# Cross attention on one Trainium2 core: values as three one-pass products, low parts of the exponents on GpSimd

## The chip, the cores and the metric

One core of one Trainium2 chip runs the whole program. The metric is the device time of one execution in microseconds (us), the median over several runs.

## The reference

Two post-norm decoder layers on x of 4 x 512 x 512 in float32: `x = layernorm(x + f(x))` for six f in turn. The change is in the fifth, the second layer's cross attention to `ctx_1024` (4 x 512 x 256), with 16 heads of 128:

```python
q = (hidden_states @ Wq).reshape(B, Sq, H, D)
k = (encoder_hidden_states @ Wk).reshape(B, Skv, H, D)
v = (encoder_hidden_states @ Wv).reshape(B, Skv, H, D)
q = rmsnorm(q, gq)
k = rmsnorm(k, gk)
scores = jnp.einsum('bqhd,bkhd->bhqk', q, k) * scale
attn = jax.nn.softmax(scores, axis=-1)
out = jnp.einsum('bhqk,bkhd->bqhd', attn, v)
return out.reshape(B, Sq, H * D) @ Wo
```

## The kernel before

`cross_attention` works on two heads at a time (`HP = 2`); with 8 such pairs in each of 4 batch entries there are N = 32 pairs, numbered j. A float32 operand `a` of most products is split into `a_hi`, rounded to float32r by ScalarE, and `a_lo = a - a_hi`, made by VectorE or GpSimd. `split3` (L196 to L200) then makes one float32 product out of three one-pass products: hi x hi, hi x lo, lo x hi. A plain float32 product takes four passes and shows as two records.

The order of the work is one list, `seq`, written out by hand in a loop over j. Every engine walks the same list and does its part of each step, so each engine's queue has the steps in the list's order. In round j three pairs are in work: the attention of pair j (`now`), the projections of pair j+1 (`nxt`) and the output of pair j-1 (`prv`). The steps are:

- E(j, h, k): scores of key block k in TensorE; ScalarE's exponent into `probs` (L1936), scaled by the keys' `rs` of GpSimd.
- U(j, h): GpSimd adds the four blocks of `probs` (L1868, L1870, L1872); SU(j, h): TensorE sums over partitions with a product by ones in bank 7 (L2111); R and M: VectorE's reciprocal (L2010) and the product with the values' result (L2015).
- V(j, h): `v` by `probs`, four float32 products (L2104) into bank 5 + h.
- Q(j, i): the two halves of the queries' projection; ScalarE squares (L1904) and copies (L1907). MQ: VectorE's mean square (a reduction L1964, a tensor_scalar L1967), then GpSimd's power -1/2 (L1843), the rstd. NQ: VectorE scales the queries in place (L1993).
- KV(j, t): keys and values of token block t; ScalarE squares, copies the keys and copies the values to `v` (L1921), which frees the bank. MK: the keys' mean square and rstd.
- TQ, TK(j, h): TensorE turns queries and keys (L2045), ScalarE takes the high part (L1925), VectorE the low part (L2000, L2003), which frees the bank.
- OH(j, h): high (L1943) and low part (L2020) of the attention's output. O(j, t): output projection, which VectorE adds to `x` (L2025).
- WQ, WK, WO: ScalarE's high parts of the next weights (L1892, L1895, L1898); GpSimd's low parts at WQ, WKl, WOl (L1849, L1853, L1857). After each low part SP loads the next weights into the one raw buffer.

Banks: Q, KV, TK and TQ take turns in banks 0 and 1, E and O in 2 to 4, V in 5 and 6, SU in 7. Before the change KV2 takes the bank of KV1, as TQ0 stands between them in the order of use:

```python
            if s[0] in ("Q", "KV", "TK", "TQ") or s[0] == "X" and s[2] % 2:
                uses.append((s, na % 2, 1))
                na += 1
```

Of the kernel before, what the change touches and what calls it, by code (L numbers as in the profile page):

```python
# [20 lines left out]
P = 128  # L21
B, S, D = 4, 512, 512
T = S // P
# [8 lines left out]
DX = 128  # L32
# [1605 lines left out]
def cross_attention(c):  # L1638
# [11 lines left out]


    nc, d, ps = c.nc, c.d, c.ps
    HP = 2
# [3 lines left out]
    with ExitStack() as ctx:  # L1657
# [21 lines left out]
        kk = sb("k", [P, T, NW])  # L1679
        v = sb("v", [P, T, NW])  # L1680
        sq = c.xcur[:, 0:2, :].rearrange("p a (b n) -> p (a b) n", n=NW)
# [4 lines left out]
        f_l = sb("qkT_lo", [P, 2, HP, S], F32R)  # L1686
        probs = sb("probsT", [P, HP, T, S])
        inv = sb("inv_sums", [P, HP, S])
        o_h = sb("outT_hi", [P, HP, S], F32R)
# [10 lines left out]
        x_hi, ctx_hi, ctx_lo = cnt("x_hi", KD), cnt("ctx_hi"), cnt("ctx_lo")  # L1700
        squared = {"q": cnt("q_squared"), "k": cnt("k_squared")}
        ms_ready = {"q": cnt("q_mean_sq"), "k": cnt("k_mean_sq")}
        rs_ready = {"q": cnt("q_rstd"), "k": cnt("k_rstd")}
        q_normed = cnt("q_normed")
        f_hi = {"TK": cnt("kT_hi", HP), "TQ": cnt("qT_hi", HP)}
        p_sum, o_hi, o_lo = cnt("probs_summed", HP), cnt("out_hi", HP), cnt("out_lo", HP)
        var_ready, rstd_ready, nmr_ready = cnt("ln_var"), cnt("ln_rstd"), cnt("ln_shift")
# [5 lines left out]
        for j in range(-1, N + 1):  # L1713
            now, nxt, prv, border = 0 <= j < N, j + 1 < N, 0 <= j - 1, (j + 2) % G == 0 and j + 2 < N
            if now:
                seq += [("E", j, 0, k) for k in range(T)] + [("U", j, 0)]
            if nxt:
                seq.append(("Q", j + 1, 0))
            if now:
                for k in range(T):  # L1720
                    seq.append(("E", j, 1, k))
                    if prv and k < HP:
                        seq.append(("OH", j - 1, k))
                seq += [("U", j, 1), ("V", j, 0)]
            elif prv:
                seq += [("OH", j - 1, h) for h in range(HP)]
            if j + 2 < N:
                seq.append(("WQ", j + 2))
            if nxt:
                if (j + 1) % G == 0 and j > 0:  # L1730
                    seq.append(("Cx", (j + 1) // G))
                seq += [("Q", j + 1, 1), ("MQ", j + 1)]
            if now:
                seq += [("SU", j, 0), ("R", j, 0)]
            if j + 2 < N:
                seq.append(("WK", j + 2))
            if now:
                seq.append(("WO", j))
            if border:
                seq += [("X", (j + 2) // G, k) for k in range(KD)]  # L1740
            if j % G == 1 and j > G:
                seq.append(("LX", j // G - 1))
            if nxt:
                seq.append(("NQ", j + 1))
            if now:
                seq.append(("M", j, 0))
            if prv:
                seq.append(("O", j - 1, 0))
            if now:
                seq.append(("V", j, 1))  # L1750
            if nxt:
                seq.append(("KV", j + 1, 0))
            if now:
                seq.append(("SU", j, 1))
            if nxt:
                seq += [("KV", j + 1, 1), ("TQ", j + 1, 0), ("KV", j + 1, 2)]
            if j + 2 < N:
                seq.append(("WKl", j + 2))
            if now:
                seq.append(("WOl", j))  # L1760
            if prv:
                seq.append(("O", j - 1, 1))
            if nxt:
                seq += [("TQ", j + 1, 1), ("KV", j + 1, 3), ("MK", j + 1)]
            if prv:
                seq.append(("O", j - 1, 2))
            if nxt:
                seq.append(("TK", j + 1, 0))
            if prv:
                seq.append(("O", j - 1, 3))  # L1770
            if nxt:
                seq.append(("TK", j + 1, 1))
            if now:
                seq += [("R", j, 1), ("M", j, 1)]
            if prv and j % G == 0:
                seq.append(("L", j // G - 1))
# [3 lines left out]
        for s in seq:  # L1780
            if s[0] in ("Q", "KV", "TK", "TQ") or s[0] == "X" and s[2] % 2:
                uses.append((s, na % 2, 1))
# [4 lines left out]
            elif s[0] == "V":  # L1787
                uses.append((s, 5 + s[2], 1))
            elif s[0] == "SU":
                uses.append((s, 7, 1))  # L1790
# [49 lines left out]
        def _(pool):  # L1840
            def rstd(i, nm, j):
                pool.wait_ge(*ms_ready[nm].after(j, 1))
                pool.tensor_tensor(rs[:, i, :, :], ms[:, i, :, :], c.mhalf[:, 0:T * HP].rearrange("p (t h) -> p t h", h=HP),  # L1843
                                   ALU.pow).then_inc(rs_ready[nm].sem, 1)

            for ph, j, *s in seq:
# [16 lines left out]
                elif ph == "U":  # L1863
# [8 lines left out]
                    pool.tensor_tensor(psum[:, h, :], psum[:, h, :], probs[:, h, 3, :], ALU.add).then_inc(p_sum.sem, 1)  # L1872
                    pool.drain()
                elif ph == "L":
                    pool.wait_ge(*var_ready.after(j, 1))
# [3 lines left out]
        def _(act):  # L1879
            for ph, j, *s in seq:  # L1880
# [15 lines left out]
                elif ph == "WO":  # L1896
                    act.wait_ge(*rawo_in.after(j, 16))
                    act.activation(side(wo_h, j), raw_o[:, :], ACT.Copy).then_inc(wo_hi.sem, 1)  # L1898
                elif ph == "Q":
                    i = s[0]  # L1900
                    act.wait_ge(*ps.full(0, ("Q", j, i)))
                    if j > 0:
                        act.wait_ge(*ms_ready["k"].after(j - 1, 1))
                    sqr = act.activation(sq[:, 2 * i:2 * i + 2, :].rearrange("p a n -> p (a n)"), ps.ap(("Q", j, i)), ACT.Square)  # L1904
                    if i == 1:
                        sqr.then_inc(squared["q"].sem, 1)
                    act.activation(q[:, 2 * i:2 * i + 2, :].rearrange("p a n -> p (a n)"), ps.ap(("Q", j, i)), ACT.Copy) \  # L1907
                       .then_inc(ps.freed(("Q", j, i)), 1)
                elif ph == "KV":
# [3 lines left out]
                    if t == 0:  # L1913
                        act.wait_ge(*ms_ready["q"].after(j, 1))
                    sqr = act.activation(sq[:, t, :], kv[:, 0:NW], ACT.Square)  # L1915
                    if t == T - 1:
                        sqr.then_inc(squared["k"].sem, 1)
                    act.activation(kk[:, t, :], kv[:, 0:NW], ACT.Copy)
                    if j > 0 and t == 0:
                        act.wait_ge(*ps.full(0, ("V", j - 1, 1)))  # L1920
                    act.activation(v[:, t, :], kv[:, NW:], ACT.Copy).then_inc(ps.freed(("KV", j, t)), 1)  # L1921
                elif ph in ("TK", "TQ"):
# [4 lines left out]
                elif ph == "E":  # L1927
                    h, k = s
                    if h == 0 and k == 0:
                        act.wait_ge(bound_ready, 1)  # L1930
                        act.wait_ge(*rs_ready["k"].after(j, 1))
                    if k == 0 and j > 0:
                        act.wait_ge(*p_sum.after(j - 1, h + 1))
                        act.wait_ge(*ps.full(0, ("V", j - 1, h)))
                    act.wait_ge(*ps.full(0, ("E", j, h, k)))
# [15 lines left out]
        def _(dve):  # L1951
# [10 lines left out]
            def mean_squares(i, nm, j):  # L1962
                dve.wait_ge(*squared[nm].after(j, 1))
                dve.tensor_reduce(ms[:, i, :, :], sq.rearrange("p t (h n) -> p t h n", h=HP), AX.X, ALU.add)  # L1964
                dve.drain()
                per = (1.0 / DX, 1e-5) if nm == "q" else (1.0, 1e-5 * DX)
                dve.tensor_scalar(ms[:, i, :, :], ms[:, i, :, :], per[0], per[1], ALU.mult, ALU.add) \  # L1967
                   .then_inc(ms_ready[nm].sem, 1)

            for ph, j, *s in seq:  # L1970
# [18 lines left out]
                elif ph == "NQ":  # L1989
                    dve.wait_ge(*rs_ready["q"].after(j, 1))  # L1990
                    dve.wait_ge(*ps.released(0, ("Q", j, 1)))
                    x3 = q[:, :, :].rearrange("p t (h n) -> p (t h) n", h=HP)
                    dve.tensor_tensor(x3, x3, rs[:, 0, :, :].rearrange("p t h -> p (t h)").unsqueeze(2)  # L1993
                                      .broadcast_to([P, T * HP, DX]), ALU.mult).then_inc(q_normed.sem, 1)
                elif ph in ("TK", "TQ"):
                    h = s[0]
# [44 lines left out]
        def _(pe):  # L2041
# [6 lines left out]
            for ph, j, *s in seq:  # L2048
# [48 lines left out]
                elif ph == "V":  # L2097
                    h = s[0]
                    ps.wait_empty(pe, 0, key)
                    if h == 0:  # L2100
                        pe.wait_ge(*ps.released(0, ("KV", j, T - 1)))
                    for k in range(T):
                        pe.wait_ge(*ps.released(0, ("E", j, h, k)))
                        mm = pe.matmul(ps.ap(key), v[:, k, h * DX:(h + 1) * DX], probs[:, h, k, :],  # L2104
                                       start=(k == 0), stop=(k == T - 1))
                    mm.then_inc(ps.filled(key), 1)
# [600 lines left out]
```

## Time and profile before

| | us |
|---|---|
| median of 3 runs | 2547.98 (2547.49 to 2548.07) |
| the profiled execution, its own time | 2548.6 |
| its span, first to last instruction | 2546.8 |
| cross attention, first to last copy of output weights (L1898, one a pair) | 1208.4 to 2246.1 |
| TensorE busy over the span | 2188.1 (86%) |
| VectorE, ScalarE, GpSimd busy over the span | 1422.8, 1224.2, 932.3 |

PE is TensorE's matmul, PEld its weight load, DVE VectorE, ACT ScalarE, POOL GpSimd, SP SyncE. Rows of a timeline give start, duration, engine, line, operation, output<-input, count, and in brackets the idle time before with what ended it. TensorE's products are pipelined and their ends are modelled, so prices of products are taken from start to start. The mean granted clock of TensorE over the span is 0.948 of full speed.

### The profile page before, as it was taken

What the parts mean: (1) busy time and instruction counts of PE and PEld (TensorE: products, weight loads), DVE (VectorE), ACT (ScalarE), POOL (GpSimd) and SP (SyncE); (2) the same over time, 40 slices, a digit from 0 to 9 for tenths busy, and PEclk for the clock granted to TensorE, in tenths of its full rate; (3) what the DMA queues carried; (4) which work ended last, traced back from release to release, by engine and by line L of the source; (5) the groups of instructions that cost most, each with busy time, mean ns of one, the idle gap of its engine ahead of it and who ended that gap; (6) DMA issues with size and microseconds to landing.
All of it is one profiled execution on the core that took longest, in us unless ns stands there. A gap on an engine that the chain in (4) does not pass through costs nothing. (4 is left out here: it accounts for less than half of the span.)

```text
span 2546.8 us, 33202 instructions
## 1 busy us (share of the span) xinstructions
PE 2188.1 (86%) x12629; PEld 1551.4 (61%) x12664; DVE 1422.8 (56%) x2129; ACT 1224.2 (48%) x2321; POOL 932.3 (37%) x662
## 2 busy tenths in 40 slices
PE   5989899857896787797999999999999999976781
PEld 4555556436675665555677777777777777753340
DVE  3656666635555435543566665566666655652637
ACT  3636464523424636544555555555555555541413
POOL 2525252410003202203555555555555655520101
PEclk9999999978997999998999999999999999988786
DMA  3000000010001000002111111111111111011001
GB/s 110 1 1 1 1 1 1 1 63 1 1 1 49 1 1 1 1 2 80 47 50 50 58 50 50 42 39 53 50 50 50 50 50 45 20 46 56 1 1 66
DMA packets 60550, 79.12 MB, mean 31 GB/s; under 512 B 6052, under 2 KB 40228, under 8 KB 60392
## 3 DMA queue, kind: packets, MB, share of 16 engines
q1 hardware_dynamic: 60392, 76.99, 9.0%
q8 instruction: 102, 1.67, 0.3%
q14 instruction: 56, 0.46, 0.1%
HBM read 72.78 MB, written 4.19 MB: 30 GB/s over the span
## 5 line engine op out<-in xcount | busy, mean ns | idle before, releaser
L2104 PE MATMUL banks<-s_probsT,s_v 128*128 128x512 f32 x512 | 230.1, 592 | 0.0
L594 DVE TENSOR_REDUCE s_neg_max<-banks 128x1 f32<-128x512 f32 x256 | 165.5, 685 | 89.4 <-PE banks L660 87.9
L2010 DVE RECIPROCAL s_inv_sums<-banks 128x512 f32<-128x512 f32 x64 | 214.2, 3347 | 1.2 <-PE banks L2111 1.2
L1843 POOL TENSOR_TENSOR s_qk_rstd<-s_mean_sq,minus_half 128x8 f32<-128x8 f32 x64 | 105.2, 1643 | 249.2 <-DVE s_mean_sq L1967 246.1
L1936 ACT ACTIVATE s_probsT<-banks,s_minus_bound,s_qk_rstd 128x512 f32<-128x512 f32 x256 | 186.3, 785 | 11.2 <-PE banks L200 11.2
L543 ACT ACTIVATE s_probsT<-banks 128x512 f32<-128x512 f32 x256 | 148.8, 600 | 81.4 <-PE banks L674 79.1
L1964 DVE TENSOR_REDUCE s_mean_sq<-x_cur 128x8 f32<-128x1024 f32 x64 | 78.1, 1220 | 185.5 <-ACT x_cur L1904 174.3
L198 PE MATMUL banks<-s_w_proj_hi,xT_hi 128*128 128x256 f32 x512 | 158.3, 309 | 2.9 <-DVE s_w_proj_lo L1987 2.9
L2104 PEld LDWEIGHTS banks<-s_probsT,s_v 128*128 128x128 f32 x512 | 96.9, 189 | 97.9 <-issue 92.4
L1915 ACT ACTIVATE x_cur<-banks 128x256 f32<-128x256 f32 x128 | 49.3, 385 | 219.3 <-PE banks L200 219.1
L1868 POOL TENSOR_TENSOR x_cur<-s_probsT 128x512 f32<-128x512 f32 x64 | 82.3, 1286 | 193.3 <-ACT s_probsT L1936 193.1
L198 PE MATMUL banks<-s_w_proj_hi,s_ctxT_hi 128*128 128x512 f32 x256 | 131.5, 514 | 19.4 <-ACT s_v L1921 19.4
L199 PE MATMUL banks<-s_w_proj_lo,xT_hi 128*128 128x256 f32 x512 | 145.8, 285 | 0.0
L200 PE MATMUL banks<-s_w_proj_hi,xT_lo 128*128 128x256 f32 x512 | 145.7, 285 | 0.0
L482 POOL TENSOR_TENSOR x_cur<-s_probsT 128x512 f32<-128x512 f32 x64 | 82.1, 1282 | 158.2 <-PE banks L692 109.9
L660 PE MATMUL banks<-s_kT,s_qT 128*128 128x512 f32 x256 | 118.4, 468 | 6.8 <-ACT s_qT L532 3.2
L2025 DVE TENSOR_TENSOR x_all<-banks,x_all 128x512 f32<-128x512 f32 x128 | 87.7, 685 | 60.3 <-PE banks L200 58.5
L1904 ACT ACTIVATE x_cur<-banks 128x512 f32<-128x512 f32 x64 | 38.2, 598 | 171.6 <-PE banks L200 171.6
L674 PE MATMUL banks<-s_qT,s_kT 128*128 128x512 f32 x256 | 106.3, 415 | 16.4 <-ACT s_qT L536 14.3
L198 PE MATMUL banks<-s_w_out_hi,s_outT_hi 128*128 128x512 f32 x256 | 115.6, 451 | 5.5 <-DVE s_outT_lo L2020 5.5
L198 PE MATMUL banks<-s_wqkv_hi,xT_hi 128*128 128x512 f32 (+1 forms) x256 | 92.1, 360 | 29.0 <-POOL s_wqkv_lo L464 8.8
L198 PE MATMUL banks<-s_qkT_hi 128*128 128x512 f32 x256 | 105.8, 413 | 2.8 <-DVE s_qkT_lo L2003 2.8
(417 smaller groups left out, 6156.5 us busy)
## 6 DMA issues: line engine op xcount, KB each, us to landing
s_w_proj_raw<-l1x_wq SPq DMA_DIRECT2D x32, 512.0 KB, 3.3
s_w_out_raw<-l1x_wo SPq DMA_DIRECT2D x32, 512.0 KB, 3.6
s_w_proj_raw<-l1x_wk SPq DMA_DIRECT2D x32, 256.0 KB, 2.8
s_w_proj_raw<-l1x_wv SPq DMA_DIRECT2D x32, 256.0 KB, 3.1
x_all<-x SPq DMA_DIRECT2D x4, 1024.0 KB, 12.7
s_ctxT<-ctxT SPq DMA_DIRECT2D x8, 512.0 KB, 4.9
out<-x_all SPq DMA_DIRECT2D x4, 1024.0 KB, 4.3
s_probsT<-l0a_wqkv SPq DMA_DIRECT2D x1, 1536.0 KB, 9.4
```

The costliest lines, as they stand in the source:

```text
L198: pe.matmul(out, lhs[0], rhs[0], start=start, stop=False)
L199: pe.matmul(out, lhs[0], rhs[1], start=False, stop=False)
L200: return pe.matmul(out, lhs[1], rhs[0], start=False, stop=stop)
L543: act.activation(probsT[:, h % NPB, k, :], ps.ap(s), ACT.Exp).then_inc(ps.freed(s), 1)
L594: dve.tensor_reduce(nmax[:, h % 2, t, 0:1], ps.ap(s), AX.X, ALU.max, negate=True) \
L660: pe.matmul(ps.ap(s), qT[:, h % NQB, t * P:(t + 1) * P], kT[:, h % NKV, :], start=True, stop=True).then_inc(ps.filled(s), 1)
L674: pe.matmul(ps.ap(s), kT[:, h % NKV, k * P:(k + 1) * P], qT[:, h % NQB, :], start=True, stop=True).then_inc(ps.filled(s), 1)
L1843: pool.tensor_tensor(rs[:, i, :, :], ms[:, i, :, :], c.mhalf[:, 0:T * HP].rearrange("p (t h) -> p t h", h=HP), ALU.pow).then_inc(rs_ready[ ...
L1936: act.activation(probs[:, h, k, :], ps.ap(("E", j, h, k)), ACT.Exp, bias=bound[:, 0:1], scale=rs[:, 1, k, h:h + 1]).then_inc(ps.freed(("E" ...
L2010: dve.reciprocal(inv[:, h, :], ps.ap(("SU", j, h))).then_inc(ps.freed(("SU", j, h)), 1)
L2025: dve.tensor_tensor(xt, ps.ap(("O", j, t)), xt, ALU.add).then_inc(ps.freed(("O", j, t)), 1)
L2104: mm = pe.matmul(ps.ap(key), v[:, k, h * DX:(h + 1) * DX], probs[:, h, k, :], start=(k == 0), stop=(k == T - 1))
```

## The change

1. The values' product becomes three one-pass products for each key block. `v` is kept as `v_hi` (ScalarE's copy) and `v_lo` (a new VectorE subtraction at KV, which now frees the bank). The exponents are kept as `probs` and, for one head at a time, `p_h` (a ScalarE copy of two blocks, 128x1024, at the new step PH) and `p_l` (a GpSimd subtraction of the same size, at the new step PL). In V the eight products with `p_h` come first, then the four with `p_l`. A head's first PH waits until the values before it in the same buffer are done.
2. U(j, 1) goes behind the second half of the queries and the rstd; WQ behind that. SU(j, 1) goes behind KV3 and MK.
3. TQ(j, 0) goes into bank 7, between the two sums.
4. Three pairs of semaphores (q and k) become one each, counted twice a round.

```diff
+        v_h = sb("v_hi", [P, T, NW], F32R)
+        v_l = sb("v_lo", [P, T, NW], F32R)
...
+        p_h = sb("probsT_hi", [P, T, S], F32R)
+        p_l = sb("probsT_lo", [P, T, S], F32R)
...
             if now:
-                seq += [("E", j, 0, k) for k in range(T)] + [("U", j, 0)]
+                for k in range(T):
+                    seq.append(("E", j, 0, k))
+                    if k % 2:
+                        seq += [("PH", j, 0, k // 2), ("PL", j, 0, k // 2)]
+                seq.append(("U", j, 0))
...
-                seq += [("U", j, 1), ("V", j, 0)]
+                seq.append(("V", j, 0))
+                for i in range(2):
+                    seq += [("PH", j, 1, i), ("PL", j, 1, i)]
             elif prv:
                 seq += [("OH", j - 1, h) for h in range(HP)]
-            if j + 2 < N:
-                seq.append(("WQ", j + 2))
             if nxt:
                 if (j + 1) % G == 0 and j > 0:
                     seq.append(("Cx", (j + 1) // G))
                 seq += [("Q", j + 1, 1), ("MQ", j + 1)]
+            if now:
+                seq.append(("U", j, 1))
+            if j + 2 < N:
+                seq.append(("WQ", j + 2))
...
-            if nxt:
-                seq.append(("KV", j + 1, 0))
-            if now:
-                seq.append(("SU", j, 1))
-            if nxt:
-                seq += [("KV", j + 1, 1), ("TQ", j + 1, 0), ("KV", j + 1, 2)]
+            if j < 0:
+                seq += [("KV", 0, 0), ("KV", 0, 1), ("KV", 0, 2), ("KV", 0, 3), ("TQ", 0, 0)]
+            elif nxt:
+                seq += [("KV", j + 1, 0), ("KV", j + 1, 1), ("TQ", j + 1, 0)]
+            if nxt and now:
+                seq.append(("KV", j + 1, 2))
...
             if nxt:
-                seq += [("TQ", j + 1, 1), ("KV", j + 1, 3), ("MK", j + 1)]
+                seq.append(("TQ", j + 1, 1))
+                if now:
+                    seq.append(("KV", j + 1, 3))
+                seq.append(("MK", j + 1))
+            if now:
+                seq.append(("SU", j, 1))
...
-            if s[0] in ("Q", "KV", "TK", "TQ") or s[0] == "X" and s[2] % 2:
+            if s[0] in ("Q", "KV", "TK") or s[0] == "TQ" and s[2] or s[0] == "X" and s[2] % 2:
...
-            elif s[0] == "SU":
+            elif s[0] in ("SU", "TQ"):
                 uses.append((s, 7, 1))
...
+                elif ph == "PL":
+                    h, i = s
+                    k2 = slice(2 * i, 2 * i + 2)
+                    pool.wait_ge(*p_hi.after(j, 2 * h + i + 1))
+                    pool.tensor_tensor(p_l[:, k2, :], probs[:, h, k2, :], p_h[:, k2, :].bitcast(F32), ALU.subtract) \
+                        .then_inc(p_lo.sem, 1)
...
+                elif ph == "PH":
+                    h, i = s
+                    k2 = slice(2 * i, 2 * i + 2)
+                    if i == 0 and j + h > 0:
+                        act.wait_ge(*ps.full(0, ("V", j, 0) if h else ("V", j - 1, 1)))
+                    act.wait_ge(*ps.released(0, ("E", j, h, 2 * i + 1)))
+                    act.activation(p_h[:, k2, :], probs[:, h, k2, :], ACT.Copy).then_inc(p_hi.sem, 1)
...
-                    act.activation(v[:, t, :], kv[:, NW:], ACT.Copy).then_inc(ps.freed(("KV", j, t)), 1)
+                    act.activation(v_h[:, t, :], kv[:, NW:], ACT.Copy).then_inc(v_hi.sem, 1)
...
                     if k == 0 and j > 0:
                         act.wait_ge(*p_sum.after(j - 1, h + 1))
-                        act.wait_ge(*ps.full(0, ("V", j - 1, h)))
+                        act.wait_ge(*p_lo.after(j - 1, 2 * h + 2))
...
+                elif ph == "KV":
+                    t = s[0]
+                    dve.wait_ge(*v_hi.after(j, t + 1))
+                    dve.tensor_tensor(v_l[:, t, :], ps.ap(("KV", j, t))[:, NW:], v_h[:, t, :].bitcast(F32), ALU.subtract) \
+                       .then_inc(ps.freed(("KV", j, t)), 1)
...
+                    cols = slice(h * DX, (h + 1) * DX)
                     for k in range(T):
-                        pe.wait_ge(*ps.released(0, ("E", j, h, k)))
-                        mm = pe.matmul(ps.ap(key), v[:, k, h * DX:(h + 1) * DX], probs[:, h, k, :],
-                                       start=(k == 0), stop=(k == T - 1))
+                        if k % 2 == 0:
+                            pe.wait_ge(*p_hi.after(j, 2 * h + k // 2 + 1))
+                        pe.matmul(ps.ap(key), v_h[:, k, cols], p_h[:, k, :], start=(k == 0), stop=False)
+                        pe.matmul(ps.ap(key), v_l[:, k, cols], p_h[:, k, :], start=False, stop=False)
+                    for k in range(T):
+                        if k % 2 == 0:
+                            pe.wait_ge(*p_lo.after(j, 2 * h + k // 2 + 1))
+                        mm = pe.matmul(ps.ap(key), v_h[:, k, cols], p_l[:, k, :], start=False, stop=(k == T - 1))
                     mm.then_inc(ps.filled(key), 1)
```

## Rows read from the trace of the kernel before

**Rows 1.** Busy time in one round: stretch, length, engines (instructions), TensorE's clock, DMA.

```profile
1799.10:1832.60 33.50, 32.91 (x157) 24.51 (x156) 19.65 (x20) 17.72 (x33) 19.04 (x12) 1.00 0.15 47
```

**Rows 2.** Line L1898: count, shortest/median/longest ns, first and last start.

```profile
L1898 ACT ACTIVATE s_w_out_hi<-s_w_out_raw x32: 1055/1056/1062, 1208.4 to 2246.1; 128x1024 fp32r<-128x1024 f32 x32
```

**Rows 3.** Timeline of TensorE in that round (start us, us, instruction, idle before).

```profile
1802.69 0.28 PE L198 MATMUL banks<-s_w_proj_hi,xT_hi 128*128 128x256 f32 x1
...
1805.56 0.40 PE L198 MATMUL banks<-s_qkT_hi 128*128 128x512 f32 x1
...
1806.26 0.40 PE L198 MATMUL banks<-s_qkT_hi 128*128 128x512 f32 x1
...
1808.38 3.59 PE L2104 MATMUL banks<-s_probsT,s_v 128*128 128x512 f32 x8
...
1811.92 0.28 PE L199 MATMUL banks<-s_w_proj_lo,xT_hi 128*128 128x256 f32 x1
...
1825.17 0.50 PE L198 MATMUL banks<-s_w_proj_hi,s_ctxT_hi 128*128 128x512 f32 x1 [0.59 <-ACT s_v L1921]
...
1833.44 0.47 PE L198 MATMUL banks<-s_qkT_hi 128*128 128x512 f32 x1
```

**Rows 4.** Timeline of ScalarE in that round.

```profile
1800.91 2.79 ACT L1936 ACTIVATE s_probsT<-banks,s_minus_bound,s_qk_rstd 128x512 f32<-128x512 f32 x4 [0.18 <-PE banks L200]
...
1814.88 0.60 ACT L1904 ACTIVATE x_cur<-banks 128x512 f32<-128x512 f32 x1 [3.37 <-PE banks L200]
...
1834.50 2.12 ACT L1936 ACTIVATE s_probsT<-banks,s_minus_bound,s_qk_rstd 128x512 f32<-128x512 f32 x3 [0.18 <-PE banks L200]
```

**Rows 5.** Timeline of VectorE in that round.

```profile
1816.80 0.56 DVE L1967 TENSOR_SCALAR s_mean_sq<-s_mean_sq 128x8 f32<-128x8 f32 x1
1817.28 3.34 DVE L2010 RECIPROCAL s_inv_sums<-banks 128x512 f32<-128x512 f32 x1
1820.54 1.96 DVE L1993 TENSOR_TENSOR s_q<-s_q,s_qk_rstd 128x1024 f32<-128x1024 f32 x1
1822.43 0.68 DVE L2015 TENSOR_TENSOR s_inv_sums<-banks,s_inv_sums 128x512 f32<-128x512 f32 x1
1823.03 0.68 DVE L2025 TENSOR_TENSOR x_all<-banks,x_all 128x512 f32<-128x512 f32 x1
...
1831.76 0.17 DVE L1967 TENSOR_SCALAR s_mean_sq<-s_mean_sq 128x8 f32<-128x8 f32 x1
```

**Rows 6.** Timeline of GpSimd in that round.

```profile
1810.64 1.27 POOL L1868 TENSOR_TENSOR x_cur<-s_probsT 128x512 f32<-128x512 f32 x1 [2.70 <-ACT s_probsT L1936]
...
1814.94 2.39 POOL L1849 TENSOR_TENSOR s_w_proj_lo<-s_w_proj_raw,s_w_proj_hi 128x1024 fp32r<-128x1024 f32 x1 [0.16 <-issue]
1817.44 1.65 POOL L1843 TENSOR_TENSOR s_qk_rstd<-s_mean_sq,minus_half 128x8 f32<-128x8 f32 x1
1819.06 2.37 POOL L1853 TENSOR_TENSOR s_w_proj_lo<-s_w_proj_raw,s_w_proj_hi 128x1024 fp32r<-128x1024 f32 x1
1821.38 3.37 POOL L1857 TENSOR_TENSOR s_w_out_lo<-s_w_out_raw,s_w_out_hi 128x1024 fp32r<-128x1024 f32 x1
1832.01 1.64 POOL L1843 TENSOR_TENSOR s_qk_rstd<-s_mean_sq,minus_half 128x8 f32<-128x8 f32 x1 [7.26 <-DVE s_mean_sq L1967]
```

**Rows 7.** Timeline of VectorE in the last pair.

```profile
2244.11 3.37 DVE L2020 TENSOR_TENSOR s_outT_lo<-s_inv_sums,s_outT_hi 128x512 fp32r<-128x512 f32 x2
```

**Rows 8.** Timeline of GpSimd in the last pair.

```profile
2245.39 1.53 POOL L1872 TENSOR_TENSOR x_cur<-x_cur,s_probsT 128x512 f32<-128x512 f32 x1
```

**Rows 9.** DMA issues: KB each, median us from issue to landing.

```profile
s_w_proj_raw<-l1x_wq SPq DMA_DIRECT2D x32, 512.0 KB, 3.3
```

**Rows 10.** Timeline of TensorE in the second pair.

```profile
1220.82 1.09 PE L2045 MATMUL banks<-ident_sb,s_k 128*128 128x128 f32 x8 [1.02 <-ACT s_v L1921]
1222.89 0.79 PE L198 MATMUL banks<-s_qkT_hi 128*128 128x512 f32 x1 [0.97 <-DVE s_qkT_lo L2003]
```

**Rows 11.** Busy time and granted clock behind that wait, columns as in rows 1.

```profile
1223.00:1226.00 3.00, 3.00 (x7) 2.37 (x8) 3.00 (x2) 0.92 (x2) 0.44 (x1) 0.50 0.00 0
```

More of the change, by code:

```diff
@@ L1679, in cross_attention @@
         kk = sb("k", [P, T, NW])
-        v = sb("v", [P, T, NW])
+        v_h = sb("v_hi", [P, T, NW], F32R)
+        v_l = sb("v_lo", [P, T, NW], F32R)
         sq = c.xcur[:, 0:2, :].rearrange("p a (b n) -> p (a b) n", n=NW)
@@ L1700, in cross_attention @@
         x_hi, ctx_hi, ctx_lo = cnt("x_hi", KD), cnt("ctx_hi"), cnt("ctx_lo")
-        squared = {"q": cnt("q_squared"), "k": cnt("k_squared")}
-        ms_ready = {"q": cnt("q_mean_sq"), "k": cnt("k_mean_sq")}
-        rs_ready = {"q": cnt("q_rstd"), "k": cnt("k_rstd")}
+        squared = cnt("qk_squared", 2)
+        ms_ready, rs_ready, nth = cnt("qk_mean_sq", 2), cnt("qk_rstd_ready", 2), {"q": 1, "k": 2}
         q_normed = cnt("q_normed")
         f_hi = {"TK": cnt("kT_hi", HP), "TQ": cnt("qT_hi", HP)}
+        p_hi, p_lo, v_hi = cnt("probs_hi", 2 * HP), cnt("probs_lo", 2 * HP), cnt("v_hi", T)
         p_sum, o_hi, o_lo = cnt("probs_summed", HP), cnt("out_hi", HP), cnt("out_lo", HP)
@@ L1841, in rstd @@
             def rstd(i, nm, j):
-                pool.wait_ge(*ms_ready[nm].after(j, 1))
+                pool.wait_ge(*ms_ready.after(j, nth[nm]))
                 pool.tensor_tensor(rs[:, i, :, :], ms[:, i, :, :], c.mhalf[:, 0:T * HP].rearrange("p (t h) -> p t h", h=HP),
-                                   ALU.pow).then_inc(rs_ready[nm].sem, 1)
+                                   ALU.pow).then_inc(rs_ready.sem, 1)
             for ph, j, *s in seq:
@@ L1902, in _ @@
                     if j > 0:
-                        act.wait_ge(*ms_ready["k"].after(j - 1, 1))
+                        act.wait_ge(*ms_ready.after(j - 1, nth["k"]))
                     sqr = act.activation(sq[:, 2 * i:2 * i + 2, :].rearrange("p a n -> p (a n)"), ps.ap(("Q", j, i)), ACT.Square)
                     if i == 1:
-                        sqr.then_inc(squared["q"].sem, 1)
+                        sqr.then_inc(squared.sem, 1)
                     act.activation(q[:, 2 * i:2 * i + 2, :].rearrange("p a n -> p (a n)"), ps.ap(("Q", j, i)), ACT.Copy) \
@@ L1913, in _ @@
                     if t == 0:
-                        act.wait_ge(*ms_ready["q"].after(j, 1))
+                        act.wait_ge(*ms_ready.after(j, nth["q"]))
                     sqr = act.activation(sq[:, t, :], kv[:, 0:NW], ACT.Square)
                     if t == T - 1:
-                        sqr.then_inc(squared["k"].sem, 1)
+                        sqr.then_inc(squared.sem, 1)
                     act.activation(kk[:, t, :], kv[:, 0:NW], ACT.Copy)
@@ L1930, in _ @@
                         act.wait_ge(bound_ready, 1)
-                        act.wait_ge(*rs_ready["k"].after(j, 1))
+                        act.wait_ge(*rs_ready.after(j, nth["k"]))
                     if k == 0 and j > 0:
                         act.wait_ge(*p_sum.after(j - 1, h + 1))
-                        act.wait_ge(*ps.full(0, ("V", j - 1, h)))
+                        act.wait_ge(*p_lo.after(j - 1, 2 * h + 2))
                     act.wait_ge(*ps.full(0, ("E", j, h, k)))
@@ L1962, in mean_squares @@
             def mean_squares(i, nm, j):
-                dve.wait_ge(*squared[nm].after(j, 1))
+                dve.wait_ge(*squared.after(j, nth[nm]))
                 dve.tensor_reduce(ms[:, i, :, :], sq.rearrange("p t (h n) -> p t h n", h=HP), AX.X, ALU.add)
@@ L1967, in mean_squares @@
                 dve.tensor_scalar(ms[:, i, :, :], ms[:, i, :, :], per[0], per[1], ALU.mult, ALU.add) \
-                   .then_inc(ms_ready[nm].sem, 1)
+                   .then_inc(ms_ready.sem, 1)
             for ph, j, *s in seq:
@@ L1989, in _ @@
                 elif ph == "NQ":
-                    dve.wait_ge(*rs_ready["q"].after(j, 1))
+                    dve.wait_ge(*rs_ready.after(j, nth["q"]))
                     dve.wait_ge(*ps.released(0, ("Q", j, 1)))
```

## The prediction

> **What bounds the kernel now.** I read the busy time of one round of the cross attention first (a round: one pair of heads; 32 pairs, 31 rounds from the first pair's to the last pair's). In 33.50 us TensorE is busy 32.91 at a granted clock of 1.00; VectorE has 19.65, ScalarE 17.72, GpSimd 19.04 [rows 1]. So TensorE sets the round. Over the stage the same line returns 31 times between 1208.4 and 2246.1, 33.5 us each [rows 2].
>
> TensorE's own timeline then gives prices as steps from start to start, since its ends are modelled [rows 3]. A half of the queries (24 products of 256 columns) takes 1805.56 - 1802.69 = 2.87 us, 0.12 each. Three one-pass products of 512 columns take 1806.26 - 1805.56 = 0.70, 0.233 each. A head's values begin at 1808.38; the second product behind them starts at 1811.92, so the values end at 1811.92 - 0.12 = 11.80 and cost **3.42 us** for 8 records, or 0.86 for 2, which is also what one sum (SU) costs. The one wait in the round is 0.59 before the third KV block.
>
> The other engines' timelines tell who could take over. I count from a pair's first exponent, 1800.91 [rows 4], in round times. In these the second Q half reaches ScalarE at 14.0, the mean square's tensor_scalar starts at 15.9, the query scaling (NQ, L1993) runs 19.6 to 21.6, and the next pair's first exponent is at 1834.50, so this round is 33.6 [rows 4, 5].
>
> **VectorE and GpSimd block each other** in these rows. The tensor_scalar, ready at 1816.80, takes 0.56 instead of the 0.17 it takes when GpSimd idles: it ends as GpSimd's subtraction of 2.39 us does. NQ starts at 1820.54 in GpSimd's L1853, which ends at 1821.43, and ends 1.07 later; GpSimd's next one, L1857, takes 3.37 where L1853 takes 2.37, so it lost 1.0 [rows 5, 6]. L2015, with one operand in PSUM, takes 0.68 in the midst of L1857: no conflict [rows 5, 6]. In the last pair two low parts of the output (L2020) meet the adds: 3.37 us for two, and the add beside them 1.53 [rows 7, 8], some 0.25 lost to GpSimd for each (1.53 against 1.27 in [rows 6]).
>
> **The change, part by part.**
>
> 1. Values on TensorE: 12 one-pass products replace a four-pass chain, 12 x 0.233 = 2.80 against 3.42, so 0.62 less a head and 1.24 a pair [rows 3]. The wait of 0.59 goes too, since queries turned in bank 7 leave KV2 another bank. TensorE alone would run at 33.5 - 1.24 - 0.59 = 31.7. Weights for the extra products load beside the products before, as those of the 0.233 steps do.
>
> 2. ScalarE copies the exponents' high parts (PH): 4 a pair, 128x1024 from SBUF, the form of L1898 at 1.06 us [rows 2]. That is 4.2 us on top of 17.72 of 33.50 [rows 1]; the engine has room. On the path only the first counts (below).
>
> 3. VectorE's four low parts of the values: no row has 128x256. The 128x512 product from PSUM is 0.68 [rows 5]; bounds are half of that and the whole, 0.34 to 0.68. I take 0.35, half of that row for half of its columns. With one operand in PSUM it meets no port [rows 5, 6]. Only KV0's lies on the path, since it frees KV2's bank; at the upper bound a round gains 0.3.
>
> 4. GpSimd's low parts of the exponents (PL): four subtractions of the form and size of L1849 and L1853, 2.37 to 2.39 us, 9.5 a pair [rows 6]. This is the large term. Old GpSimd stood idle 7.26 before the keys' rstd and 2.70 before the second sum [rows 6].
>
> 5. Moved: U1 (three adds, 1814.94 - 1810.64 = 4.30 us [rows 6]) goes behind the queries' rstd, so WQ, WKl, WOl run later. SP waits for each of these before it loads the next weights; a load lands after 3.3 us [rows 9], and ScalarE wants it most of a round later: nothing. WQ's copy on ScalarE goes behind Q1: nothing. SU1 goes behind KV3, 0.86 inside the stretch from KV2 to the next scores. The merged semaphores cost nothing, as the waits are the same.
>
> **GpSimd's order, added up.** From the first exponent: two exponents (2.79 for four [rows 4], some 1.45 for two) and the first PH (1.06) pass before PL can start, at 2.6. Then PL, PL 4.75; U0 4.3; PL, PL 4.75; a wait of 0.2 for the tensor_scalar; queries' rstd 1.62; U1 4.3; WQ, WKl, WOl 7.1; keys' rstd 1.62. Sum 31.2. With the port's losses (two L2020 at 0.25, NQ 1.0, tensor_scalar 0.2) it is 32.9. So GpSimd is full as well, and whoever of VectorE wants the port finds it taken.
>
> **The chain I forecast.** V0 starts at 7.5 as before and ends at 10.3 (PL01 ends at 7.45, in time). Q1 reaches ScalarE 3.08 after V0's end, as 1814.88 - 1811.80 [rows 3, 4], at 13.35, and the tensor_scalar is ready 1.92 later (1816.80 - 1814.88 [rows 4, 5]), at 15.3. GpSimd has U0 from 7.45 to 12.25 (with 0.5 lost), PL10 to 14.6, PL11 to 17.0. The tensor_scalar misses the gap at 14.6 by 0.7 and stands until 17.0. Behind it in VectorE's queue is the reciprocal, 3.26 to the next start [rows 5], 17.1 to 20.4, and then NQ. U1's adds run from 18.85 (rstd 17.2 to 18.85), the second from 20.3: NQ finds the port taken just before it, waits to 21.6 and ends at 22.65. KV2 needs KV0's bank, whose low part stands in VectorE's queue behind NQ, M0 and O0: 0.6 + 0.6 (L2015 to the next start [rows 5]) + 0.35, and 0.15 to TensorE (less than half of the 0.36 by which 1834.50 - 1833.44 exceeds three products), so KV2 starts at 24.4. TensorE was through KV1 at 20.8 (PL11 at 17.0, four products, two KV blocks of 1.4), and stands except for one turn. From KV2 to the next scores it took 1833.44 - 1825.17 = 8.27; with SU1 9.13; from scores to exponent 1834.50 - 1833.44 = 1.06 [rows 3, 4]. Round: 24.4 + 9.13 + 1.06 = **34.6**, against 33.6: 1.0 longer.
>
> Bounds: if NQ slips in ahead of the second add it is 1.1 earlier, but then the keys' tensor_scalar (ready at 30.8) stands behind WOl (to 31.3), the keys' low parts behind it, and the round is 34.0. With the values' low part at 0.68 it is 34.9. So 34.0 to 34.9; I take 34.6, nearest to the rows' order. 31 rounds x 1.0 = 31 us. The execution profiled took 2548.6 (span 2546.8, 1.8 around it), 0.6 above the median of 2547.98. Forecast 2548.6 + 31 = **2580**, own range 2561 to 2592.
>
> **Rivals.**
>
> *TensorE stays the bound (faster).* If the port conflicts fall into GpSimd's gaps and the tensor_scalar gets in before PL11, the round is between TensorE's 31.7 and GpSimd's 32.9; at 32.5 the time is 2548.6 - 31 x 1.1 = 2514. For it: TensorE has by far the most work, and the sum of GpSimd's order is below 33.6. Against: GpSimd leaves no gap in which VectorE could go first. It decides from the point where NQ ends before 33.6 - (34.6 - 22.65) = 21.65 and the keys' tensor_scalar no longer waits behind WOl. Chance 0.16.
>
> *Even.* GpSimd's order plus a little of the chain, 33.4 to 33.7; the gain on TensorE is given back exactly: 2542 to 2552. Chance 0.12.
>
> *The clock falls in the new wait.* In the second pair TensorE stood 1.02 and 0.97 us around eight turns, and the granted clock behind was 0.50 for 3 us [rows 10, 11], that is 1.2 of 2.4 GHz. The wait from 20.8 to 24.4, with four turns in it, is like that one. Three us at half speed lose 1.5, so with one in each round 36.1 and 2548.6 + 31 x 2.5 = 2626. Against: the 0.59 waits of each old round leave the clock at 1.00 [rows 1, 3]. Chance 0.20.
> The Trainium skill ("TensorE: Matmul & The Clock Gate", Part 1) says that half speed is the default state and only activity lifts it; by that rule a stand of this kind in every round would cost in every round, and the time would be the 2626 of this rival. The trace of before has the one case.
>
> *The exponents' low parts are slower than L1853,* or the one buffer for both heads holds the second head back: PL10 waits for V0's end (10.3 + 0.2 + 1.06 = 11.6) but GpSimd is in U0 until 12.25, so this costs nothing until V0 is 0.7 late. It is within the forecast's range.
>
> **How the numbers follow.** Chances: forecast 0.52, clock 0.20, faster 0.16, even 0.12. 0.2% (5 us) is about what a measurement of this kernel can tell from no change. Faster is 0.16, same 0.12, slower 0.52 + 0.20 = 0.72. The range goes down to 2530, which leaves out most of the faster case (0.12), and up to 2640, one and a half of the clock's falls in some rounds, which leaves out 0.06.
>
> **What would show it.** Right: L2104's successors in steps of 0.23; GpSimd near 29 us busy a round; the queries' tensor_scalar (L1967) far above the 0.56 of [rows 5], ending with PL11; NQ ending 22 to 23 after the first exponent; TensorE waiting before the queries' turn and KV2 for VectorE; a round of 34 to 35. Wrong: a round below 33.3 with NQ early, or GpSimd idle for several us before the keys' rstd. The clock rival shows as a granted clock clearly below 1.00 in the stage.

## The result, and the profile after

| | before | changed |
|---|---|---|
| median, us | 2548.03 | 2571.51 (2570.22 to 2572.57) |
| span of the profiled execution | 2546.8 | 2570.8 |
| first to last L1898 (L1921 after) | 1208.4 to 2246.1 | 1210.9 to 2268.1 |

The change makes the kernel slower: ratio 1.0092, interval 1.0074 to 1.0109, +23.5 us against a forecast of +31. Of the 24.0 us in the span, 19.5 lie in the 31 rounds (34.10 us instead of 33.47 on average, the line of [rows 2] in both traces), 2.5 ahead of the first and 2.0 behind the last.

The rounds are not alike, and the average hides it. Taken one by one from ScalarE's timelines, from one start of L1898 (L1921) to the next:

| rounds | before, us | changed, us | longer by, in all |
|---|---|---|---|
| 19 ordinary ones, median | 33.56 | 33.80 | 4.3 |
| 9 around the three changes of batch entry, sum | 309.2 | 319.0 | 9.9 |
| the first and the last two, sum | 90.7 | 96.2 | 5.5 |

An ordinary round is only 0.24 longer, and the one read below is ordinary: 33.78 from first exponent to first exponent. Its busy time comes first, as in [rows 1].

```profile
1812.03:1845.81 33.78, 32.31 (x166) 26.01 (x165) 22.75 (x24) 21.85 (x37) 29.38 (x15) 1.00 0.15 48
```

GpSimd went from 19.04 to 29.38 us. TensorE stands for 1.5 of 33.78 (0.6 of 33.50 before). Now the same round in timelines: TensorE around the values and the waits (to set beside [rows 3]),

```profile
1819.56 0.39 PE L2141 MATMUL banks<-s_probsT_hi,s_v_hi 128*128 128x512 f32 x1
...
1822.34 0.28 PE L198 MATMUL banks<-s_w_proj_hi,xT_hi 128*128 128x256 f32 x1
...
1833.72 0.65 PE L2080 MATMUL banks<-ident_sb,s_q 128*128 128x128 f32 x4 [0.51 <-DVE s_q L2023]
...
1835.24 0.50 PE L198 MATMUL banks<-s_w_proj_hi,s_ctxT_hi 128*128 128x512 f32 x1 [0.87 <-DVE s_v_lo L2028]
...
1844.73 0.50 PE L198 MATMUL banks<-s_qkT_hi 128*128 128x512 f32 x1
```

VectorE (beside [rows 5]),

```profile
1827.34 1.99 DVE L1997 TENSOR_SCALAR s_mean_sq<-s_mean_sq 128x8 f32<-128x8 f32 x1
1829.24 3.34 DVE L2045 RECIPROCAL s_inv_sums<-banks 128x512 f32<-128x512 f32 x1
1832.51 1.16 DVE L2023 TENSOR_TENSOR s_q<-s_q,s_qk_rstd 128x1024 f32<-128x1024 f32 x1
...
1834.78 0.74 DVE L2028 TENSOR_TENSOR s_v_lo<-banks,s_v_hi 128x256 fp32r<-128x256 f32 x2
...
1842.76 0.72 DVE L1997 TENSOR_SCALAR s_mean_sq<-s_mean_sq 128x8 f32<-128x8 f32 x1
...
1844.00 0.67 DVE L2038 TENSOR_TENSOR s_qkT_lo<-banks,s_qkT_hi 128x512 fp32r<-128x512 f32 x1
```

and GpSimd (beside [rows 6]).

```profile
1814.71 4.83 POOL L1895 TENSOR_TENSOR s_probsT_lo<-s_probsT,s_probsT_hi 128x1024 fp32r<-128x1024 f32 x2 [3.28 <-ACT s_probsT_hi L1928]
1819.50 1.74 POOL L1885 TENSOR_TENSOR x_cur<-s_probsT 128x512 f32<-128x512 f32 x1
...
1824.55 4.76 POOL L1895 TENSOR_TENSOR s_probsT_lo<-s_probsT,s_probsT_hi 128x1024 fp32r<-128x1024 f32 x2 [0.16 <-ACT s_probsT_hi L1928]
...
1831.02 1.29 POOL L1885 TENSOR_TENSOR x_cur<-s_probsT 128x512 f32<-128x512 f32 x1
1832.45 2.34 POOL L1887 TENSOR_TENSOR x_cur<-x_cur,s_probsT 128x512 f32<-128x512 f32 x1
...
1841.07 2.39 POOL L1874 TENSOR_TENSOR s_w_out_lo<-s_w_out_raw,s_w_out_hi 128x1024 fp32r<-128x1024 f32 x1
```

The queries' tensor_scalar, an operation of 0.17, is ready at 1827.34 and ends at 1829.33, as GpSimd's two low parts end (1824.55 + 4.76 = 1829.31). The reciprocal and the query scaling (L2023) follow in VectorE's queue. TensorE waits 0.51 for the scaling before it turns the queries, and 0.87 for KV0's low part before KV2. GpSimd's second add takes 2.34 instead of 1.29 while the scaling takes 1.16: I read this as the scaling going first. The port, here and below, is whatever the two engines can't use at the same time in such rows.

The keys' tensor_scalar stands until WOl ends (1841.07 + 2.39 = 1843.46; it ends at 1843.48). Behind it in VectorE's queue come an add of the output and the turned keys' low part, which ends at 1844.67; the next scores start at 1844.73, and the next exponent at 1845.81. GpSimd, from its first low part at 1814.71 to the end of WOl, never pauses for more than 0.16. So this round is closed by GpSimd's order and the keys' tensor_scalar behind it; whether the wait ahead of KV2 counts as well is for the runs below to say.

At the changes of batch entry something more happened. TensorE's two waits are longer there; this is the second change:

```profile
1730.02 0.66 PE L2080 MATMUL banks<-ident_sb,s_q 128*128 128x128 f32 x4 [0.84 <-DVE s_q L2023]
1731.55 0.73 PE L198 MATMUL banks<-s_w_proj_hi,s_ctxT_hi 128*128 128x512 f32 x1 [0.87 <-DVE s_v_lo L2028]
```

and behind them the granted clock (third from the end of the row) is 0.50, the lower of the two levels, 1.2 of 2.4 GHz:

```profile
1732.00:1735.00 3.00, 3.00 (x8) 2.34 (x7) 0.48 (x1) 0.55 (x3) 2.84 (x3) 0.50 0.00 0
```

It fell in the same place at the third change (0.50 from 2009 to 2011) and not at the first, where the waits are 0.82 and 0.87. These two rounds take 35.97 and 35.95 us, the same round at the first change 34.81: some 1.15 for each fall.

### The profile page after: what moved, and what is told of

The parts are those of the page before. It is cut to its first block and busy times, and to the rows that moved or that the text cites. A ratio compares the mean times of both kernels' runs of the same rounds, so it can differ in the third digit from the quotient of the medians.

```text
span 2570.8 us, 34161 instructions
## 1 busy us (share of the span) xinstructions
PE 2170.7 (84%) x12885; PEld 1600.1 (62%) x12920; DVE 1520.8 (59%) x2257; ACT 1355.2 (53%) x2449; POOL 1264.9 (49%) x790
## 5 line engine op out<-in xcount | busy, mean ns | idle before, releaser
L1895 POOL TENSOR_TENSOR s_probsT_lo<-s_probsT,s_probsT_hi 128x1024 fp32r<-128x1024 f32 x128 | 309.2, 2427 | 105.4 <-ACT s_probsT_hi L1928 103.1
L482 POOL TENSOR_TENSOR x_cur<-s_probsT 128x512 f32<-128x512 f32 x64 | 82.1, 1283 | 158.4 <-PE banks L692 110.0
L1928 ACT ACTIVATE s_probsT_hi<-s_probsT 128x1024 fp32r<-128x1024 f32 x128 | 132.1, 1056 | 30.7 <-PE banks L2146 26.5
L198 PE MATMUL banks<-s_w_proj_hi,xT_hi 128*128 128x256 f32 x512 | 145.8, 285 | 2.9 <-DVE s_w_proj_lo L2017 2.9
L198 PE MATMUL banks<-s_w_proj_hi,s_ctxT_hi 128*128 128x512 f32 x256 | 108.7, 425 | 38.3 <-DVE s_v_lo L2028 33.2
L198 PE MATMUL banks<-s_w_out_hi,s_outT_hi 128*128 128x512 f32 x256 | 128.4, 502 | 5.5 <-DVE s_outT_lo L2055 5.5
L2055 DVE TENSOR_TENSOR s_outT_lo<-s_inv_sums,s_outT_hi 128x512 fp32r<-128x512 f32 x64 | 70.9, 1109 | 95.8 <-ACT s_outT_hi L1973 95.7
L1887 POOL TENSOR_TENSOR x_cur<-x_cur,s_probsT 128x512 f32<-128x512 f32 x64 | 119.6, 1868 | 9.7 <-issue 0.9
L926 POOL TENSOR_TENSOR s_ln_rstd<-s_ln_var_eps,minus_half 128x4 f32<-128x4 f32 x8 | 8.1, 1008 | 198.7 <-DVE s_ln_var_eps L998 198.7
```

The lines of the kernel that those rows point to most:

```text
L198: pe.matmul(out, lhs[0], rhs[0], start=start, stop=False)
L1895: pool.tensor_tensor(p_l[:, k2, :], probs[:, h, k2, :], p_h[:, k2, :].bitcast(F32), ALU.subtract) \
L1928: act.activation(p_h[:, k2, :], probs[:, h, k2, :], ACT.Copy).then_inc(p_hi.sem, 1)
```

## The experiments

All edits are against the changed kernel, and all ratios against the kernel before, run on the same chip. "An ordinary round" is the median of the same 19 rounds in the run's trace: 33.56 us before, 33.80 in the changed kernel.

**The low parts on VectorE** (`e_low_dve`).

```diff
-                    pool.tensor_tensor(p_l[:, k2, :], probs[:, h, k2, :], p_h[:, k2, :].bitcast(F32), ALU.subtract) \
...
+                    dve.tensor_tensor(p_l[:, k2, :], probs[:, h, k2, :], p_h[:, k2, :].bitcast(F32), ALU.subtract) \
```

> The changed kernel with one difference: the exponents' low parts (PL) are made by VectorE instead of GpSimd. Theory (GpSimd's 9.5 us of low parts fill that engine and make VectorE's tensor_scalar and query scaling wait for the port, which lengthens the chain from the first exponent to the third KV block): GpSimd falls back to about 19 us a round, the round from 34.1 to 32 to 32.9 us, the time to some 2521 (2502 to 2533), faster than both kernels. Rival (the new order costs: sums behind the last keys, turned queries in the sums' bank, ScalarE's copies): within 10 us of the changed kernel's 2571. Second rival (VectorE, with 4.5 us more a round, becomes the bound): 2571 or more.

2514.11 us, ratio 0.9863 (0.9849 to 0.9878). Same instructions, another engine: 57 us less than the changed kernel. Its mean-square tensor_scalar and scaling:

```profile
1827.27 0.17 DVE L1991 TENSOR_SCALAR s_mean_sq<-s_mean_sq 128x8 f32<-128x8 f32 x1
...
1830.65 1.16 DVE L2017 TENSOR_TENSOR s_q<-s_q,s_qk_rstd 128x1024 f32<-128x1024 f32 x1
```

The pair's first exponent is at 1811.95 there, so the tensor_scalar ends at 15.5 instead of 17.3 and the scaling at 19.9 instead of 21.6. An ordinary round is 32.05. VectorE has 439.81 of 500 us (1400 to 1900); TensorE waited for it a little (9.2 us in all from 1300 to 2200).

**Half of it** (`e_half_low`): the second head's low parts on VectorE, the first head's on GpSimd.

```diff
-                elif ph == "PL":
+                elif ph == "PL" and s[0] == 0:
...
+                elif ph == "PL" and s[0] == 1:
...
+                    dve.tensor_tensor(p_l[:, k2, :], probs[:, h, k2, :], p_h[:, k2, :].bitcast(F32), ALU.subtract) \
```

> The changed kernel with the second head's two low parts of the exponents on VectorE, the first head's on GpSimd. Theory (GpSimd's fill and its hold on the port at the tensor_scalar): GpSimd at about 24 us a round, PL11 no longer before the tensor_scalar; the round is 32.2 to 32.9, 2525 (2510 to 2535), most of the gain of moving all four. Rival (each low part moved gives the same): half of 57 us, 2543.

2529.14 us, ratio 0.9928 (0.9914 to 0.9943), an ordinary round 32.51: 42 of the 57 us come with the half that lies ahead of the tensor_scalar. The gain is not in proportion.

**No subtraction after the first head's** (`e_stale_low`): the buffer keeps that head's low parts, so the output lacks the right ones.

```diff
+                    if j == 0 and h == 0:
+                        pool.tensor_tensor(p_l[:, k2, :], probs[:, h, k2, :], p_h[:, k2, :].bitcast(F32), ALU.subtract) \
...
+                    else:
+                        pool.nop().then_inc(p_lo.sem, 1)
```

> The changed kernel with the subtraction of the exponents' low parts left out after the first head (the buffer keeps that head's; GpSimd only signals), so the output lacks the right low parts of the exponents; all products and copies stay. Theory (the subtractions are what costs, on whichever engine): TensorE sets the round at 31.8 us as in the best run, 2505 (2495 to 2515), at or below the run with the low parts on VectorE, 2514. Rival (VectorE's queue ahead of KV2 still binds when GpSimd is free): 2530 to 2545.

2508.03 us, ratio 0.9840 (0.9825 to 0.9854), an ordinary round 32.04. VectorE's queue has the same operations as in the changed kernel and hardly binds any more: the subtractions on GpSimd cost 63 us.

**The order alone** (`e_order`): `v` in float32, no PH and PL.

```diff
-                        pe.matmul(ps.ap(key), v_h[:, k, cols], p_h[:, k, :], start=(k == 0), stop=False)
...
+                        mm = pe.matmul(ps.ap(key), v[:, k, cols], probs[:, h, k, :], start=(k == 0), stop=(k == T - 1))
```

> The new order of steps alone: sums behind the last keys, turned queries in bank 7, second sum of exponents behind the queries' rstd, but the values as four-pass float32 products and no high or low parts of exponents and values. Theory (the new order is sound and frees the 0.59 us wait at KV2; what costs is GpSimd's low parts): TensorE sets the round at 33.5 - 0.6 = 32.9, time 2530 (2525 to 2548). Rival (the new order itself costs): above 2552.

2517.66 us, ratio 0.9878 (0.9861 to 0.9894): better than expected, outside its range. From 1400 to 1900 TensorE is busy without a gap (columns as in [rows 1]):

```profile
1400.00:1900.00 500.00, 499.97 (x2378) 373.94 (x2377) 314.49 (x318) 278.38 (x517) 290.42 (x171) 1.00 0.16 50
```

Before, it was 490.64 in the same stretch. So the order is worth 30 us by itself, and what is added to it in the change costs 54.

**The order with the low parts made and not used** (`e_dead_low`): as above, but PH and PL stay, with their waits.

```diff
+                        if k == T - 1:
+                            pe.wait_ge(*p_lo.after(j, 2 * h + 2))
+                        mm = pe.matmul(ps.ap(key), v[:, k, cols], probs[:, h, k, :], start=(k == 0), stop=(k == T - 1))
```

> The new order with four-pass float32 values, as in the run of the order alone, but with the exponents' high parts on ScalarE and low parts on GpSimd still made, in their places and with their waits; TensorE's products don't read them. Theory (GpSimd's four subtractions by themselves turn the gain of the order into a loss, because GpSimd's order with its port losses is a floor of 33.4 to 33.9 us a round): 2558 (2548 to 2572), some 40 us above the order alone at 2518. Rival (it is the one-pass values' own waits, the bank of KV2 held by VectorE's low part of the values, that cost): 2518 to 2530.

2555.82 us, ratio 1.0027 (1.0018 to 1.0037): 38 us above the order alone. The exponents' high and low parts, with their waits, cost this with no change to the values and with KV2's bank freed by ScalarE. GpSimd is busy 434.94 of 500 us. An ordinary round is 33.77, as in the changed kernel (33.80): there the one-pass values gain nothing, though TensorE's products for them are shorter. The 16 us between the two runs lie ahead of the first round (7) and around the changes of batch entry (8); what causes them there was not tried.

**No tensor_scalar on VectorE** (`e_no_ts`): ScalarE squares with a scale, GpSimd adds the epsilon.

```diff
-                dve.tensor_scalar(ms[:, i, :, :], ms[:, i, :, :], per[0], per[1], ALU.mult, ALU.add) \
...
+                pool.tensor_scalar(ms[:, i, :, :], ms[:, i, :, :], 1e-5 if nm == "q" else 1e-5 * DX, None, ALU.add)
```

> The changed kernel without VectorE's tensor_scalar on the mean squares: ScalarE squares with a scale, GpSimd adds the epsilon ahead of its power (two small GpSimd instructions more a round), so VectorE's reciprocal no longer stands behind PL11 for the port. Theory (the port wait of the tensor_scalar, 1.99 us in the traced round, is a link of the chain): the reciprocal starts at 15.3 instead of 17.2 after the first exponent, the query scaling is ready when the rstd is, and a round is 0.3 to 1.2 us shorter: 2534 to 2562, I take 2550. Rival (GpSimd's own work is the bound): the extra instructions lengthen the round by 0.3 to 1 us each, 2590 to 2620.

2564.12 us, ratio 1.0060 (1.0045 to 1.0075): 7 less than the changed kernel, although GpSimd has more to do; two us outside the range I gave. An ordinary round is 33.54. The granted clock fell at all three changes of batch entry in this run's trace.

**M and O of the first head later in VectorE's queue** (`e_m0_late`).

```diff
+            dseq, held = [], []
+            for st in seq:
+                if st[0] == "M" and st[2] == 0 or st[0] == "O" and st[2] == 0:
+                    held.append(st)
+                    continue
...
-            for ph, j, *s in seq:
+            for ph, j, *s in dseq:
```

> The changed kernel with one difference, on VectorE's queue alone: the product M of the first head and the add of the first output block (0.6 us each) go behind the low part of KV1, so they no longer stand between the query scaling and KV0's low part, which frees the bank of the third KV block. Theory (the chain through VectorE's queue sets the round): KV2 starts up to 1.2 us earlier, the round goes from 34.1 to about 33.2, where GpSimd's order takes over; 2543 (2536 to 2555). Rival (GpSimd's throughput sets the round already): 2571 within 4.

2565.02 us, ratio 1.0064 (1.0049 to 1.0079): 6.5 less, a quarter of what I expected and outside the ranges of theory and rival alike. In an ordinary round it gained nothing, 33.83 against 33.80: the wait went elsewhere. KV2 no longer waits, the keys' mean square comes earlier and stands longer behind WOl:

```profile
1803.16 1.88 DVE L1997 TENSOR_SCALAR s_mean_sq<-s_mean_sq 128x8 f32<-128x8 f32 x1
...
1805.56 0.68 DVE L2050 TENSOR_TENSOR s_qkT_lo<-banks,s_qkT_hi 128x512 fp32r<-128x512 f32 x1
```

and TensorE's scores wait for the turned keys' low part behind it:

```profile
1806.29 0.50 PE L198 MATMUL banks<-s_qkT_hi 128*128 128x512 f32 x1 [1.26 <-DVE s_qkT_lo L2050]
```

So the wait ahead of KV2 did not set the ordinary round. The gain lies ahead of the first round (2.3), around the changes of batch entry (4.3, where the clock does not fall in this run) and in the last two rounds (1.1).

**Both at once** (`e_both`).

> Both changes of the two single runs at once, low parts still on GpSimd: no tensor_scalar on VectorE, and M and O of the first head behind KV1's low part. Theory now (each of the two frees a link of VectorE's chain, then GpSimd's own order with its port losses takes over: from the trace with M late 5.0 us from the keys' tensor_scalar to the first low part, 4.8, 5.05, 4.87, 1.6, 5.4, 7.1, with the first term down to 4.6): a round of 33.4 us, 2551 (2545 to 2556), not faster than the kernel before beyond its noise. Rival (the gains of the two add without a floor, 6.5 and 7.4 us): 2557. Rival (no GpSimd floor, TensorE takes over): 2500 to 2515.

2551.06 us, ratio 1.0014 (1.0004 to 1.0024), as expected: 20 us together, more than the 14 of the two alone. In an ordinary round M and O later add nothing where the tensor_scalar is gone (33.57 against 33.54). What the two gain together beyond their sum is around the changes of batch entry: those nine rounds sum to 305.5 us (changed kernel 319.0, without the tensor_scalar 316.0, with M and O later 314.7), and the clock does not fall there. GpSimd's order is what is left, 445.07 of 500 us busy: the first exponent waits for GpSimd's rstd of the keys.

```profile
1833.95 1.45 ACT L1968 ACTIVATE s_probsT<-banks,s_minus_bound,s_qk_rstd 128x512 f32<-128x512 f32 x2 [1.49 <-POOL s_qk_rstd L1862]
```

**The low parts on VectorE with these** (`e_low_m0` with M and O later; `e_all` with both).

> All low parts of the exponents on VectorE, and M and O of the first head behind KV1's low part. Theory (with GpSimd free TensorE sets the round, 32.1 us in the traced round with hardly a wait left): little is left to gain, 2511 (2506 to 2515). Rival (VectorE's chain still sets it): 2485 to 2500.

> As the run before, and no tensor_scalar on VectorE. Theory (TensorE sets the round): 2508 (2500 to 2515), equal to the run before within 5. Rival (the tensor_scalar's port wait at the keys, 0.8 us in the traced round, still counts): 2485 to 2500.

2514.15 (0.9870, 0.9855 to 0.9885) and 2506.82 us (0.9841, 0.9827 to 0.9856). The first gains nothing on `e_low_dve`, as TensorE had hardly a wait left. The second gains 7, within the range I gave for each but at 7.3 apart not within the 5: a tensor_scalar still counted for something, I take it the keys', as the queries' took 0.17 in `e_low_dve`. `e_all` is the fastest that was run, 41 us under the kernel before; an ordinary round is 31.83, where the prediction put TensorE alone at 31.7. Of its 500 us TensorE is busy 496.78.

## Why the prediction was right, point by point

The direction and the cause were right, and the total came out near the forecast partly by luck. The sum was 31 equal rounds, each 1.0 longer. An ordinary round became 0.24 longer, under even the lower bound of 34.0, and most of the 24 us came from places that the sum did not treat: the changes of batch entry (9.9), the first and last rounds (5.5), and ahead of and behind them (4.5).

Times from the first exponent, 1812.03, of the round above:

| step | forecast | measured |
|---|---|---|
| V0 ends | 10.3 | 10.31 |
| tensor_scalar ready, ends | 15.3, 17.0 | 15.31, 17.30 |
| queries' scaling starts | 20.4 | 20.48 |
| ends | 22.65 | 21.64 |
| KV2 starts | 24.4 | 23.2 |
| next first exponent | 34.6 | 33.78 |

- **Bound and mechanism.** GpSimd filled up to 29.4 us and held the port where VectorE's tensor_scalar wanted it. Taking the low parts off GpSimd (`e_low_dve`, `e_stale_low`) and adding them, with the high parts, to the order alone (`e_dead_low`) show it from both sides; `e_no_ts` shows the tensor_scalar as one link.
- **The term that was mis-sized** is the wait of the scaling for U1's second add. I put it behind that add, to end at 22.65; the scaling started 0.06 after the add's recorded start (1832.51, 1832.45) and ended at 21.64. That is the case that I had named for the bound of 34.0, with its second half too: the keys' tensor_scalar stands behind WOl, and the round is 33.78.
- **The link that was wrong** for an ordinary round is the one from the scaling over KV2 to the next scores. TensorE does wait there, 0.51 and 0.87, but `e_m0_late` took the second wait away and the round stayed as it was. What closes the round is GpSimd's order with VectorE's work on the keys behind it. By size it lies between the forecast and the rival "Even" (GpSimd's order plus a little of the chain, 33.4 to 33.7).
- **Left out of the sum:** 2.5 us ahead of the first and 2.0 behind the last L1921, since I counted rounds alone, and the rounds at the changes of batch entry, which I took for ordinary ones. The range's upper end also doesn't follow: 31 rounds at 34.9 against 33.6 give 2589, not 2592.
- **GpSimd's order** was put at 31.2, and 32.9 with the port's losses. In `e_both`, where GpSimd is what is left, an ordinary round is 33.57, some 0.8 of it for the two small tensor_scalars that the changed kernel has not on GpSimd (0.39 and 0.41 from their start to the power's). That leaves 32.8, an estimate, close to what I put. In the changed kernel the first add after the low parts takes 1.74 and the second 1.56 where 1.29 is free, 0.7 for the two L2055 as against the 0.5 I took. The first low part starts 2.68 after the first exponent (2.6 taken); but 0.60 more passes between the keys' rstd and that exponent (0.08 in `e_both`), which the sum had at nothing.
- **The order's gain** was put at 0.59 a round; in `e_order` an ordinary round is 32.74, 0.82 less, and 4.4 us are saved ahead of the first round's L1908. Where the other 0.23 come from was not looked for.
- **TensorE's price** held: V takes 1822.34 - 1819.56 = 2.78, forecast 2.80, old 3.42.
- **Rivals.** The faster one needed no port conflict. Even: `e_both` is this case made by hand. The clock rival came in two rounds of 31, at some 1.15 us each, and not in every one (the fall in the second pair is in both kernels): in an ordinary round the granted clock is 1.00, although TensorE stands 0.51 and 0.87 around four turns. The low part of the values takes 0.42 (half of 0.68 was a little too little), inside its bounds.
- **Open:** next to the order alone, one-pass values with low parts on VectorE give 4 to 11 us, not the 40 that 32 x 1.24 promises. An ordinary round of `e_all` is 0.9 under that of `e_order` (31.83, 32.74). Lost again are 6.8 us ahead of the first round's copy of output weights (1210.8 against 1204.0) and 3.7 in the last two rounds (58.9 against 55.2). The causes were not looked for.

## What to carry to other kernels

Before work is moved to an engine that looks half idle, add up its order over one round, waits included, and put into the sum who shares its port: an operation of 0.17 us took 2 here, and the reciprocal and the scaling behind it in VectorE's queue came as much later. When removing one wait gives little, look in the next trace for the wait that took its place before dropping the idea: here two edits of 7 us gave 20 together. Run the parts of a change apart; this one was a gain of 30 us and a loss of 54. And before an average round is compared with a forecast, look at the rounds one by one: here 19 of 31 were nearly as before.

## What the runs showed of the hardware

- When VectorE and GpSimd come to the port within 0.06 us of each other (scaling 1832.51, add recorded at 1832.45), VectorE went first by their lengths: the scaling took 1.16, the add 2.34. VectorE waiting behind a running operation of GpSimd also got in ahead of the next one, in the kernel before: the scaling that waited in L1853 ended 1.07 after it, and L1857, next in GpSimd's queue, took 3.37 instead of 2.37 [rows 5, 6].
- GpSimd's 128x8 tensor_scalar, one addition, costs 0.24 us, the following power 1.67, so the epsilon is cheap to add there (`e_all`):

```profile
1823.27 0.24 POOL L1860 TENSOR_SCALAR s_mean_sq<-s_mean_sq 128x8 f32<-128x8 f32 x1 [5.54 <-DVE s_mean_sq L1990]
1823.66 1.67 POOL L1862 TENSOR_TENSOR s_qk_rstd<-s_mean_sq,minus_half 128x8 f32<-128x8 f32 x1
```

- Waits of 0.51 and 0.87 us around four turns left the granted clock at 1.00 in every ordinary round; 0.84 and 0.87 around four were followed by 0.50 at two changes of batch entry, 0.82 and 0.87 at the first were not; in the second pair of the kernel before, 1.02 and 0.97 around eight had been followed by 0.50 [rows 10, 11].
